# A one-core layer of channel attention and sixteen experts: the routing choice made in pieces of 8, 8 and 16 tiles, and the dense work listed in a new order around it

## The reference, cut to what matters

```python
x = L0_attn_x                              # (16, 256, 128) float32
xn = _layernorm(x, axis=-1)
x = x + attn(xn, Wq, Wk, Wv) + ffn(xn, ...)

def attn(x, Wq, Wk, Wv):                   # 16 heads of 8
    diag_scores = einsum('cthd,cthd->cth', q, k) / sqrt(E)
    probs = softmax(diag_scores, axis=0)   # over the 16 channels c
    return probs[..., None] * v.sum(axis=1)[:, None, :, :]

def ffn(x, ...):
    scores = softmax(xf @ gate_w + gate_b)
    top_vals, top_idx = top_k(scores, 2)   # 2 of 16 experts for each token
    h = einsum('td,edh->teh', xf, w1) + b1 # each expert 128 -> 176 -> 128
    g = einsum('td,edh->teh', xf, w3) + b3
    y = einsum('teh,ehd,te->td', silu(h) * g, w2, cw) + cw @ b2
    z = silu(xf @ sw1 + sb1) * (xf @ sw3 + sb3) @ sw2 + sb2   # shared, 128 -> 352 -> 128
    return y + z
```

## Time and profile before

| | us |
|---|---|
| time, median of 3 runs | 283.98 (282.92 to 284.85) |
| span of the profiled execution | 275.7 |
| PE busy | 217.2 (79%) |
| DVE busy | 155.8 (57%) |
| POOL busy | 156.0 (57%) |
| ACT busy | 100.9 (37%) |

### The profile page before, as it was taken

How to read it: one execution, slowest core, us unless ns; L and a number is a source line. 1 busy time by engine, 2 the same in 40 slices (tenths; PEclk the granted TensorE clock), 3 DMA queues, 4 the chain that set the end, 5 groups by cost and what they waited for, 6 DMA issues and landing times.

```text
span 275.7 us, 4667 instructions
## 1 busy us (share of the span) xinstructions
PE 217.2 (79%) x1289; PEld 174.1 (63%) x1289; DVE 155.8 (57%) x423; ACT 100.9 (37%) x220; POOL 156.0 (57%) x169
## 2 busy tenths in 40 slices
PE   8989995987909969958598876977685995986860
PEld 6655683744706736457597775877675994986730
DVE  5998838689426934722366653555441452376562
ACT  2378854032013522511344432333441443434400
POOL 7238675674754760747255654556455564655573
PEclk9999979899865999988689999999999798999995
DMA  6999997112353243111122333233222358527256
GB/s 209 350 398 288 209 210 196 54 55 92 123 162 118 85 125 89 55 34 54 36 81 81 92 84 92 73 83 84 69 82 82 89 144 223 161 74 262 76 193 228
DMA packets 28397, 36.48 MB, mean 132 GB/s; under 512 B 5123, under 2 KB 23811, under 8 KB 28019
## 3 DMA queue, kind: packets, MB, share of 16 engines
q1 hardware_dynamic: 22724, 22.87, 28.4%
q0 software_dynamic: 5104, 12.79, 15.7%
q10 hardware_dynamic: 544, 0.52, 0.5%
HBM read 21.81 MB, written 14.35 MB: 131 GB/s over the span
## 4 chain that ended last, share of the span: by engine, by line
PE 40%; another core or an unknown queue 24%; DVE 14%; issue 13%; ACT 7%; DMA 1%; DVEq 0%; ACTq 0%
PE PS L1092 6%; PE PS L1214 6%; PE PS L1069 6%; PE PS L1070 6%; PE PS L1244 4%; DVE XR L515 3%; DVE sS L819 2%; PE PS L1229 2%; ACT prod L995 2%; DVE rxl L814 2%; PE PS L1201 2%; ACT sS L1001 2%; PE PS L1038 2%; PE PS L1057 2%
## 5 line engine op out<-in xcount | busy, mean ns | idle before, releaser
L490 POOL DMA_INDIRECT ydram<-fw x79 | 77.3, 979 | 60.5 <-DVE fw L823 39.0
L481 POOL DMA_INDIRECT xslot<-XR,idx x64 | 63.4, 990 | 42.7 <-issue 18.2
L1244 PE MATMUL PS<-fw,sS 89*128 (+1 forms) x316 | 44.0, 284 | 0.0
L1244 PEld LDWEIGHTS PS<-fw,sS 89*128 89x128 f32 (+1 forms) x316 | 40.6, 200 | 0.1
L823 DVE TENSOR_TENSOR fw<-PS,fw 128x256 f32<-128x256 f32 (+1 forms) x40 | 16.8, 419 | 35.1 <-remote 17.4
L1229 PE MATMUL PS<-kc,sS 128*88 128x128 f32 x158 | 25.1, 283 | 14.3 <-DVE sS L819 9.2
L1092 PEld LDWEIGHTS PS<-sw,sS 128*128 128x128 f32 (+1 forms) x192 | 27.5, 229 | 12.5 <-issue 12.5
L1092 PE MATMUL PS<-sw,sS 128*128 128x128 f32 (+1 forms) x192 | 28.3, 315 | 8.6 <-issue 5.8
L990 ACT ACTIVATE rxh<-PS 128x256 fp32r<-128x256 f32 (+1 forms) x40 | 15.2, 381 | 54.0 <-remote 31.2
L819 DVE TENSOR_TENSOR sS<-prod,PS 128x352 f32<-128x352 f32 (+1 forms) x40 | 20.6, 514 | 24.3 <-ACT prod L995 19.8
L1214 PE MATMUL PS<-w13h,rxh 128*128 x79 | 29.9, 379 | 0.8 <-DVE rxl L814 0.8
(11 more groups left out here) (147 smaller groups left out, 318.3 us busy)
## 6 DMA issues: line engine op xcount, KB each, us to landing
fw<-xslot SPq DMA_DIRECT2D x79, 72.0 KB, 1.9
fw<-wdram SPq DMA_DIRECT2D x1, 2816.0 KB, 11.4
fw<-in_w POOLq DMA_DIRECT2D x1, 2816.0 KB
X<-in_x SPq DMA_DIRECT2D x8, 256.0 KB, 5.2
XR<-ydram SPq DMA_DIRECT2D x4, 512.0 KB, 3.7
fw<-in_w SPq DMA_DIRECT2D x1, 1536.0 KB
xnT<-ydram SPq DMA_DIRECT2D x3, 512.0 KB, 4.5
out<-X SPq DMA_DIRECT2D x5, 256.0 KB
```

Source lines behind the costliest of these rows:

```text
L481: pool.indirect_dma_start(xslot, bass.IndirectOffsetOnAxis(ap=idx[:, k, t:t + 1], axis=0), XR[:, t, :], None).then_inc(d_sc[k][h][q], 16)
L490: pool.indirect_dma_start(ydram, bass.IndirectOffsetOnAxis(ap=RX[:, v, TOK:TOK + 1].bitcast(I32), axis=0), yb[:, v, :], None).then_inc(d_y ...
L1244: ins = pe.matmul(PS[:, DN_BANK[b], i * P:(i + 1) * P], raT[0:n, b, (2 * i + k) * P:(2 * i + k + 1) * P], w2[0:n, bass.ds(e * 2 * P + k * ...
```

## The change

Three things change in the dense phase, none in the slot loop or the tail.

1. The choice is made for three pieces, `PIECES`: tiles 0 to 7, 8 to 15 and 16 to 31. The first two stand right behind the norms of groups 0 to 3. The statistics of groups 4 to 7, which stood ahead of the first choice, now stand behind the second, their norms, transposes and logits among the dense work, and the third piece's choice behind `gated_up(3, 2)`.
2. The dense work is listed anew on TensorE, VectorE and ScalarE. Other PSUM banks are used (`turn_bank`, `up_banks`, `z_bank`): transposes of groups 4 to 7 share bank 0, which `turn` waits for. GpSimd norms group 3 in place of groups 4 and 5.
3. The scatters keep their order by expert and tiles in the main, and their waits become one table of 22, one for each of the first 22 `up` products; the waits for `s_y` and `s_z` go. The accumulating DMA of the expert weights (`w13`) is issued behind the eighth scatter in place of ahead of the first.

```diff
-POOLED = (4, 5)
+POOLED = (3,)
 HT = NT // 2
+PIECES = ((0, 8), (8, 8), (16, 16))
...
-PACE_UP = {0: 4, 1: 5, 4: 6, 14: 8, 18: 9, 20: 10, 23: 11, 25: 12, 27: 13, 42: 16, 43: 17, 48: 18, 49: 19, 54: 20, 56: 21, 58: 22, 59: 23, 62: 24}
-PACE_Y = {12: 1, 17: 2, 22: 3, 28: 4, 29: 5, 34: 6, 35: 7, 37: 8}
-PACE_Z = {10: 1, 16: 2, 39: 4, 46: 5, 52: 6}
...
+PACE_UP = {1: 1, 4: 2, 6: 3, 9: 4, 12: 5, 14: 6, 17: 7, 19: 8, 22: 9, 24: 10, 27: 11, 29: 12, 32: 13, 34: 14, 37: 15, 40: 16, 42: 17, 45: 18, 47: 19, 50: 20, 52: 21, 55: 22}
...
+        def turn_bank(g):
+            return g % 2 if g < 4 else 0
...
+        def scatter(n, k, u):
...
+                h, q = u // 2, u % 2
+                for t in range(u * QT, (u + 1) * QT):
+                    if n + t - u * QT in PACE_UP:
+                        pool.wait_ge(s_up, PACE_UP[n + t - u * QT])
+                    pool.indirect_dma_start(xslot, bass.IndirectOffsetOnAxis(ap=idx[:, k, t:t + 1], axis=0),
+                                            XR[:, t, :], None).then_inc(d_sc[k][h][q], 16)
...
+            pool.wait_ge(s_idx, 1)
+            pool.wait_ge(s_cw, 1)
+            scatter(0, 0, 0)
             pool.wait_ge(d_wb, 16)
             pool.dma_start(w13, d["w13"], accum_op=ALU.add, max_dma_last_dim=NBIAS).then_inc(d_wa, 16)
...
+            scatter(8, 0, 1)
+            pool.wait_ge(s_alt, 2)
+            scatter(16, 1, 0)
+            pool.wait_ge(s_idx, 4)
+            pool.wait_ge(s_alt, 4)
+            scatter(24, 1, 1)
+            pool.wait_ge(s_idx, 5)
+            pool.wait_ge(s_cw, 5)
+            scatter(32, 0, 2)
...
-                if g >= 2:
+                if g >= 4:
+                    pe.wait_ge(s_xt, 2 * g)
+                elif g >= 2:
                     pe.wait_ge(s_xt, 2 * g - 2)
```

More of the change, by code:

```diff
@@ L485, in _ @@
+            pool.wait_ge(s_alt, 8)
+            scatter(56, 1, 3)
             for p in range(NP):
@@ L606, in _ @@
             index(0, 0)
-            invert(3)
-            norm(6)
-            norm(7)
             index(1, 0)
-            dve.wait_ge(k_bh, 1)
-            dve.tensor_tensor(blo[:], braw[:], bhi[:].bitcast(F32), ALU.subtract).then_inc(k_bl, 1)
+            first(1)
+            second(1)
+            third(1)
+            rank(1)
+            weigh(1)
+            index(0, 1)
+            index(1, 1)
             def slot_table():
@@ L738, in shares @@
                 dve.wait_ge(d_vb, 16)
+            stats(4)
             gated(0, 0)
-            first(1)
+            stats(5)
+            stats(6)
+            stats(7)
+            gated(1, 1)
+            invert(2)
+            norm(4)
             add_z(0)
-            second(1)
-            gated(1, 1)
-            weigh(1)
+            norm(5)
             gated_up(2, 0)
-            third(1)
+            dve.wait_ge(k_bh, 1)
+            dve.tensor_tensor(blo[:], braw[:], bhi[:].bitcast(F32), ALU.subtract).then_inc(k_bl, 1)
             gated_up(2, 1)
-            rank(1)
+            second_place(0, 0)
+            invert(3)
+            norm(6)
             add_z(1)
+            gated_up(2, 2)
+            norm(7)
+            gated_up(3, 0)
+            gated_up(3, 1)
+            second_place(0, 1)
+            gated_up(3, 2)
+            first(2)
+            second(2)
+            third(2)
+            rank(2)
+            add_z(2)
+            weigh(2)
+            gated_up(4, 0)
+            index(0, 2)
+            index(1, 2)
             score(0)
-            second_place(0, 0)
-            index(0, 1)
-            index(1, 1)
             tally(0)
-            gated_up(2, 2)
+            gated_up(4, 1)
             split(0)
-            gated_up(3, 0)
+            add_z(3)
             score(1)
             tally(1)
-            gated_up(3, 1)
+            gated_up(4, 2)
             split(1)
+            slot_table()
+            gated_up(5, 0)
             score(2)
-            slot_table()
-            second_place(0, 1)
-            gated_up(3, 2)
             split(2)
-            score(3)
             slots()
             final_waits()
+            gated_up(5, 1)
             tally(2)
+            score(3)
+            tally(3)
+            gated_up(5, 2)
+            split(3)
             score(4)
-            tally(3)
             tally(4)
-            split(3)
-            add_z(2)
-            gated_up(4, 0)
-            gated_up(4, 1)
+            add_z(4)
             score(5)
+            gated_up(6, 0)
+            tally(5)
             score(6)
-            tally(5)
-            gated_up(4, 2)
+            split(4)
+            gated_up(6, 1)
             tally(6)
@@ L1069, in up @@
                 pe.matmul(PS[0:m, k, :], sw1[:, f:f + m], xv, start=True, stop=True)
[L1070 removed]
+                pe.matmul(PS[0:m, l, :], sw3[:, f:f + m], xv, start=True, stop=True).then_inc(s_up, 1)
             def early(n):
@@ L1106, in _ @@
             turn(2)
+            early(1)
             turn(3)
-            early(1)
+            bias(1)
             logits(2)
+            rank(0)
             logits(3)
@@ L1112, in _ @@
             early(3)
-            turn(4)
             early(4)
-            bias(1)
-            logits(4)
-            turn(5)
-            rank(0)
+            rank(1)
             early(5)
-            logits(5)
-            turn(6)
-            turn(7)
-            logits(6)
-            logits(7)
-            pe.wait_ge(k_wbd, 1)
-            pe.wait_ge(s_xt, 2 * NG)
-            pe.matmul(PS[:, 0, 0:P], wbd[:, 0, :], wbd[:, 1, :], start=True, stop=True).then_inc(k_mbd, 1)
-            pe.matmul(PS[0:C, 1, 0:P], xsum[:], wbd[:, 2, :], start=True, stop=True).then_inc(s_v, 1)
             pe.wait_ge(s_sg, 4 * NB)
```

393 lines of the change are left out of this document (203 added, 190 removed).

## The result

| | before | after |
|---|---|---|
| time, median (us) | 283.45 (282.84 to 284.85) | 292.09 (289.4 to 298.35) |
| ratio to before | | 1.027 (1.019 to 1.035) |
| span of the profiled execution | 275.7 | 288.8 |
| time of that execution | not recorded | 290.69 |
| last `index` ends | 56.2 | 85.5 |

The change makes the kernel slower: by 8.6 us in the medians, and by 2.7% in the ratio. The forecast was 289, slower.

A forecast was written before the change was run, and what follows sets the result against it. VectorE's waits ahead of the slot loop, not its work, were taken to bound the kernel. `split(10)` 112.5 + 13 of holds = 125.5, 8.5 later; first steps 3.3 off: +5.2; span 280.9 plus 8.3 gives 289, range 277 to 295.

The forecast's parts named there:

- Scatter 0 and down(0): Early choices in 8-tile operations of 0.3 us: scatter 0 from 29.34 to about 20, `down(0)` at about 31.
- The last choice, nothing held: Chain of TensorE and ScalarE for groups 4 to 7: last logits 57.7, last `index` 72.6, 16.4 us later.
- The rest of VectorE's list: From last `index` to `split(10)`: 36 us busy plus 4 of waits, ending at 112.5, 4.5 before today's 117.0.
- The holds: TensorE's signals held in unbroken scatter runs, on `up(2, 1)`, `up(3, 1)` and `logits(7)`: 4.3 + 4.7 + 3.6, rounded 13 us.
- First steps of the loop: `add_z(6)` starts 0.5 to 1.5 us behind `split(10)` instead of 4.7; entry to the slot loop 3.3 us off.
- The loop: The slot loop is not touched; only when it gets under way counts, so it has no term.
- From span to time: The time adds 8.3 us to the profiled span of 275.7; predicted span 280.9 so gives 289.
- Signals pass: 276, faster: Rival: table waits stop GpSimd often enough, under 5 us of holds; -4.5 - 3.3 = -7.8, time 276; chance 0.22.
- Their own lateness: Rival: the wait is TensorE's own, modelled ends being estimates; +10.6, time 294.6; chance 0.18 together with holds going on later.

The follow-up runs named there:

- e4_paced: Changed kernel with its wait table rewritten so each wait names the product due when GpSimd arrives; 278.69 us, 0.990 of the kernel before.
- e5_filler: Changed kernel plus a GpSimd computation behind each of scatters 16 to 23, on a chip without held signals; 238.32 us, kernel before 218.95.
- e1_gap16: Changed kernel with scatter 16 waiting for the twelfth `up` product and the four waits between 16 and 24 removed; 291.17 us, ratio 1.026.
- e2_no_waits: Changed kernel with the table emptied, so no scatter waits for an `up` product; 297.36 us.
- e3_table_alone: Kernel before, lists untouched, with the changed kernel's table of 22 waits in place of its three tables; 283.2 us, ratio 1.001.
- the first four experiments: e1_gap16, e2_no_waits, e3_table_alone and e4_paced, run on the chip that holds signals, where the kernel before takes 283 us.

## Why the prediction was right, and where it was right by luck

The forecast was 289 with slower at 0.49; the time is 292.09. The sign holds, and so does the reason given for it: GpSimd trails the new table, runs go unbroken, and products in the chain are seen late; e4_paced, which changes only the waits, takes the whole loss back. The size is luck in good part. One hold of the three forecast came, and errors of both signs met in the sum.

**Scatter 0 and down(0).** Predicted near 20 and 31; 20.34 and 32.19. The 8-tile operation was taken at 0.3 us and is 0.32 from start to start. Right, and as expected it bought nothing.

**The last choice, nothing held.** (The 64.4 on the way should read 64.6; the 72.6 fits that.) The step that put the first operation of the choice at 57.7 and the last `index` at 72.6 was too low. Without holds e5_filler has them at 60.7 and 79.5. Of the 6.9 us, 3.0 come before the choice. 1.9 lie in `down(3)`, 4.55 us at a granted 0.63 for the 2.7 of the earlier trace rows, and 1.3 in the load of the Silu table ahead of `gates(4, 0)`, which the sum left out (1.28 at 80.92 above, and in e5_filler as well); the rest is small waits. The Trainium skill (ScalarE: Activation LUTs, What ACT_TABLE_LOAD costs) gives about 1283 ns for such a load; the trace agrees with 1.28. The about 1380 ns of draining that the section adds for each switch are not seen here: the Silu starts at 82.22, 1.30 behind the start of the load.

**The clock.** Both products and choice were summed with rows at full speed. The chain makes TensorE wait, and behind its waits it runs at the lower clock: 6.15 us from `turn(7)` to the end of `up(3, 2)` in the changed kernel, where `turn(6)`, `logits(5)` and `up(3, 1)` just ahead of the hold take 3.2. It need not happen at each wait: in e1_gap16 the same three as in the first case, behind a wait of 1.60 us, take 3.2 at a granted 1.00 (55.25 to 58.46). A chain that alternates between two engines should have its products priced at both levels.

**The rest of VectorE's list.** Predicted 40 us from `index` to `split(10)`; 40.3 in e5_filler. In the changed kernel 42.9, with two waits that e5_filler hasn't, 1.93 us ahead of 93.27 and 1.52 ahead of 99.01, in and behind the run from 84.75 to 97.4. Right.

**The holds.** Predicted three, 4.3 + 4.7 + 3.6, together 13. There was one in the chain. `up(3, 1)` ended at 51.56 and was expected to be seen at 55.8; its Silu comes at 55.91, in a pair with that of `up(3, 0)`, which the step did not have among the held and which had ended at 48.5. That 55.8 fits is luck as well: the run stops 1.5 us earlier than the step's 55, and the signal comes 2.4 us behind it where about 1 had been assumed. `up(2, 1)` passed, 6.3 us into its run, and `logits(7)`, 7.8 us into a run that began at 58.96. So "longer than about 5 us" is too simple: in e4_paced a product 5.1 us into the run of 125.16 (it ends at 130.28 on TensorE's timeline) was taken up by ScalarE only at 136.65. And not every signal waits for the end of a run: VectorE goes on at 93.27, while the scatters last to 97.4. The pause at scatter 16 that the step counted on (42 to 45) did not come, since VectorE's exchange was done by 42.2, so that one run lasted from 32.23 to 53.55. By `split(10)`, held signals and what goes with them cost 128.3 - 119.7 = 8.6 us against e5_filler, which ran on another chip, and 6.7 against e4_paced. By the first number the 13 was too high by 4.4, the lists too low by 7.2 (119.7 for 112.5), and `split(10)` came at 128.3 for 125.5.

**First steps of the loop.** Predicted 3.3 us off. From `split(10)` to the first result scatter it was 21.3 us and is 18.9: 2.4 off. `add_z(6)` starts 2.6 us behind `split(10)`, not within 1.5, since `down(6)` did not end before VectorE was through: it took 4.38 us, at a granted 0.63, and ended at 130.86.

**The loop.** Taken as unchanged; from the first result scatter to the end it takes 4.2 us more. The busy time by stretch has a lower clock (the column ahead of the DMA share: 0.96 and 0.91 before, 0.90 and 0.88 after), before and then after:

```profile
134.00:205.00 71.00, 58.23 (x418) 53.84 (x419) 37.94 (x95) 28.49 (x65) 37.64 (x39) 0.96 0.28 80
205.00:290.00 85.00, 50.48 (x350) 46.13 (x348) 32.06 (x78) 22.86 (x52) 39.67 (x41) 0.91 0.41 125
```
```profile
134.00:205.00 71.00, 56.69 (x388) 52.47 (x387) 36.62 (x91) 25.80 (x58) 39.13 (x42) 0.90 0.26 75
205.00:290.00 85.00, 62.81 (x407) 56.27 (x405) 35.53 (x87) 26.79 (x60) 44.21 (x46) 0.88 0.44 136
```

The stretches are not the same part of the loop. Counted from the first result scatter to the end, TensorE is busy 104.7 us at 0.95 before and 112.1 us at 0.90 after, for 750 and 742 matmul records, so the same work. The 4.2 need not be the change's doing: e2_no_waits and e4_paced, with the changed lists and the same loop, take 137.7 us (at 0.91) and 137.2 (at 0.96) there, e3_table_alone with the lists of before 139.3 (at 0.89), and the kernel before had spans from 278.4 to 284.7 in its 13 executions beside the first four experiments.

**From span to time.** The 8.3 us between the span of 275.7 and the median of 283.98 were added to the sum as if they lay around the span. They don't: every execution with both numbers has 1.75 to 1.95 us there (290.69 for 288.8, 277.87 for 276.0, 281.0 for 279.2). By that the profiled execution of the kernel before, whose own time was not recorded, took about 277.6 us (an estimate), 6 less than its median and less than any recorded one on the first chip (280.26 and more). So every stage that is compared with its trace is compared with an uncommonly short execution. Predicted span 280.9, measured 288.8, 7.9 us short; predicted surplus 8.3, measured 1.9, 6.4 us too much. The two together are why 289 lies so near 290.69.

**The rivals.** "Signals pass: 276, faster" counted on a table that stops GpSimd often enough. The table doesn't; e4_paced is what one that does would give, 278.69. The rival's text leaves out that the held signals of before stay in its sum: where they pass in both, before takes 219 and the new lists 238. "Their own lateness" draws on the Trainium skill (Perfetto Trace Analysis, Tensor Engine Instruction), by which the end of a matmul in a profile is an estimate. In e1_gap16 two products are seen within 0.1 us of their modelled ends, so the estimate does not account for the 4.3 us; the spread-out matmuls shown there are lateness of another kind.

**What the change is worth, in all.** On chips that hold nothing the lists cost 19 us. Where signals are held, the kernel before enters the loop some 18 us later than on the other chips (`split(10)` 117.0 against 98.7), and has waits of 18.4 us in the earlier trace rows. That the holds are what makes these 18 us is argued from the two chips; no experiment took them out of the kernel before on the chip that has them. It would explain why new lists with fewer holds come out level there (e4_paced), and the same lists with a table that GpSimd reaches too late 3% behind.

## What to carry to other kernels

A wait that only paces an engine is worth something where that engine would arrive ahead of what the wait names: when the lists move, look for the paced engine at each wait on the timeline, and rename the waits or they become dead. Price a chain that alternates between engines at the lower clock too, and with the table loads that its order of functions brings. Never take the gap between one profiled span and the median of other executions for a fixed cost, and try a change on more than one chip before it is kept.
